# Delta on 32-partition blocks, three modulation rows at once, an earlier second-norm guess in a one-core Mamba and expert layer

## The reference, cut to what matters

```python
mod = (silu(c) @ wmod).reshape(4, 6, 1, -1)          # six rows of 512 per batch
sa, ca, ga, sb, cb, gb = (mod[:, i] for i in range(6))
h = layernorm(x) * (1 + ca) + sa
# the mixer
x_conv = causal_depthwise_conv(h, conv_w, conv_b)     # 4 taps
p = h @ Wxproj.T                                      # 2*128 + 1 columns
B, C = p[..., :128], p[..., 128:256]
delta = softplus(p[..., 256:])                        # one number per token
deltaA = exp(-exp(A_log) * delta)                     # 128 states
Bu = delta * B * (x_conv @ Winproj.T)
hs = scan(deltaA, Bu)                                 # hs[t] = deltaA[t]*hs[t-1] + Bu[t]
x = x + ga * ((C * hs) @ Woutproj.T + D * x_conv)     # ga clamped to |ga| >= 0.25
# the experts: each token goes to one of two
h = layernorm(x) * (1 + cb) + sb
x = x + gb * top_weight * expert[argmax](h)           # fc to 2048, leaky square, proj to 512
```

## Time and profile before

| | |
|---|---|
| time, median of 3 runs | 548.8 us (548.78 to 552.28) |
| the profiled execution | 548.64 us |
| its span, first to last instruction | 546.9 us |
| TensorE busy, share of the span | 508.2 us, 93% |
| VectorE busy | 351.1 us, 64% |
| ScalarE busy | 261.2 us, 48% |
| GpSimd busy | 159.4 us, 29% |
| mean granted TensorE clock | 0.974 |

### The profile page before, as it was taken

The page is one execution under the profiler, slowest core; times in us unless marked ns, Lnnn a source line. Parts: engine busy times, 40 slices in busy tenths (PEclk is TensorE's granted clock), DMA queues, the critical chain, the costliest instruction groups (busy, mean ns, idle before and its releaser), DMA issues.

```text
span 546.9 us, 7697 instructions
## 1 busy us (share of the span) xinstructions
PE 508.2 (93%) x2280; PEld 387.3 (71%) x2280; DVE 351.1 (64%) x734; ACT 261.2 (48%) x520; POOL 159.4 (29%) x204
## 2 busy tenths in 40 slices
PE   7899899999398999999999999999999999999990
PEld 1354355545276888898888888888888888988880
DVE  4688999898998675464445354545454544668781
ACT  2763387946786743443443344344346334433220
POOL 1100003030334520330150033034004304868583
PEclk9999999999778999999999999999999999999995
DMA  8930442220042004030022022002102300467692
GB/s 297 427 126 0 139 171 77 78 78 1 2 135 99 4 3 156 20 136 2 1 78 79 1 78 79 1 1 91 67 1 78 117 1 4 115 120 179 81 164 96
DMA packets 15729, 46.29 MB, mean 85 GB/s; under 512 B 5223, under 2 KB 5223, under 8 KB 12344
## 3 DMA queue, kind: packets, MB, share of 16 engines
q1 hardware_dynamic: 10600, 34.71, 17.8%
q0 software_dynamic: 5072, 10.79, 9.5%
HBM read 37.30 MB, written 8.71 MB: 84 GB/s over the span
## 4 chain that ended last, share of the span: by engine, by line
PE 71%; DVE 18%; issue 4%; ACT 3%; DMA 1%; DVEq 1%; POOL 1%; ACTq 0%; SPq 0%; POOLq 0%
PE bank L1200 34%; PE bank L1169 32%; DVE xc L1327 4%; DVE res L1365 2%; DVE st L1372 1%; PE bank L992 1%; DMA x_in<-x 1%; DVE st L1309 1%; ACT XSfull L769 1%; DVE eabs L1389 1%; DVE hs L1355 1%; PE bank L1006 1%; PE bank L1016 1%; DVE XSfull L1607 1%; PE bank L1033 1%
## 5 line engine op out<-in xcount | busy, mean ns | idle before, releaser
L565 POOL TENSOR_TENSOR Wlo<-raw,Whi (+1 forms) x60 | 76.3, 1301 | 227.7 <-ACT Whi L911 219.1
L1630 DVE TENSOR_TENSOR acc<-acc,bank 128x512 f32<-128x512 f32 x110 | 74.9, 687 | 57.2 <-PE bank L1200 57.2
L1614 DVE TENSOR_TENSOR twice_h<-twice_h,bank 128x512 f32<-128x512 f32 (+2 forms) x80 | 48.2, 606 | 95.5 <-ACT twice_h L882 95.5
L1169 PE MATMUL bank<-XShi,Wlo 128*128 x304 | 108.1, 355 | 0.0
L1169 PE MATMUL bank<-XSlo,Whi 128*128 x304 | 108.0, 355 | 0.0
L1169 PE MATMUL bank<-XShi,Whi 128*128 x304 | 108.0, 355 | 0.0
L1200 PE MATMUL bank<-Whi,ahi 128*128 128x512 f32 x268 | 105.2, 393 | 2.1 <-DVE alo L1620 2.1
L1200 PE MATMUL bank<-Wlo,ahi 128*128 128x512 f32 x268 | 105.2, 393 | 0.0
L1200 PE MATMUL bank<-Whi,alo 128*128 128x512 f32 x268 | 104.9, 392 | 0.0
L891 ACT ACTIVATE ahi<-twice_h 128x512 fp32r<-128x512 f32 (+2 forms) x78 | 44.6, 572 | 118.9 <-PE bank L1200 118.9
L882 ACT ACTIVATE twice_h<-bank 128x512 f32<-128x512 f32 (+2 forms) x78 | 41.4, 534 | 85.5 <-PE bank L1169 76.2
(11 more groups left out here) (197 smaller groups left out, 579.1 us busy)
## 6 DMA issues: line engine op xcount, KB each, us to landing
raw<-wffn SPq DMA_DIRECT2D x16, 1024.0 KB, 5.2
wm<-wmod SPq DMA_DIRECT2D x6, 1024.0 KB, 12.8
out<-res SPq DMA_DIRECT2D x4, 1024.0 KB, 4.5
x_in<-x SPq DMA_DIRECT2D x3, 1024.0 KB, 12.3
ga_bc<-ga_rows SPq DMA_DIRECT2D x4, 256.0 KB, 3.6
x<-x SPq DMA_DIRECT2D x1, 1024.0 KB, 5.3
bc<-router_rows_scaled SPq DMA_DIRECT2D x4, 256.0 KB, 3.6
wx_sb<-wx SPq DMA_DIRECT2D x1, 514.0 KB, 8.5
```

The source lines that it names most:

```text
L565: pool.tensor_tensor(Wlo[:, hb % 2, c, :], raw[:, c, :], Whi[:, hb % 2, c, :].bitcast(F32), ALU.subtract).then_inc(s_wlo, 1)
L1169: mm = pe.matmul(hP[(par + u) % 2][m][:, c0:c1], W[wp][:, par, 2 * e + k // 2, o:o + P], XS[xp][:, k, bass.ds(start_row[u] + c0, c1 - c0)] ...
L1614: dve.tensor_tensor(twice_h[:, m, 0:w], twice_h[:, m, 0:w], hP[(par + u) % 2][m][:, 0:w], ALU.add).then_inc(s_q2[m], 1)
L1630: dve.tensor_tensor(acc[:, n, :], acc[:, n, :], yP[s][:, :], ALU.add).then_inc(s_yu, 1)
```

## The change: what it does

1. `delta_product` puts the 512 tokens of a batch on four blocks of 32 partitions: 16 matmuls of 32x128, each at a column group of its own, into the first 128 columns of `pD`. Its weights are the column of `Wxproj` read with step 0, so `wdb` and the instructions that build it are gone.
2. Abs, Exp, `w1`, the residue, Ln and the two last steps work on 128x128 and end in `sp`.
3. A new `spread_delta` on TensorE: four matmuls of 128x128, with one column of the identity repeated as weights, take each block of `sp` back to all partitions in `pD`. ScalarE copies `pD` into `delta`, now a tile of its own, ahead of the exp in `decay`.
4. `last_mod_rows` makes rows 3, 4 and 5 together, in turns over `k`, at column groups 0, 32 and 64 of one bank. The single rows 3, 4 and 5 go. `turn(3)` moves behind `C_product(1)`; `mod_columns` for both move ahead of `softplus(1)` on VectorE.
5. On ScalarE `exp_minus_abs(1)` moves ahead of `guess1(2)`, `normalize1(2)` behind two of the row copies, and `guess2(1)` and `guess2(2)` between the last two blocks of `place`.
6. On TensorE `spread_delta(b + 1)` stands behind the state product of that batch, and the delta product of batch 3 moves from the end of batch 1's turn to between the second and third skip product of batch 2.

```diff
-        lw = take("lw", [P, L])
-        delta = lw
+        delta = take("delta", [P, L])
...
-        row_bank = (pO[0], pX, pO[0], pT[0], pT[1], pO[1])
-        col_bank = (pO[1], pO[1], pO[1], pT[0], pT[1])
+        row_bank = (pO[0], pX, pO[0], pT[0], pT[0], pT[0])
+        row_tile = (0, 0, 0, 0, 32, 64)
+        col_bank = (pO[1], pO[1], pO[1], pT[1], pT[1])
...
-                act.activation(eabs[:, :], pD[:, :], ACT.Abs).then_inc(s_ab, 1)
+                act.activation(eabs[:, 0:P], pD[:, 0:P], ACT.Abs).then_inc(s_ab, 1)
                 act.wait_ge(s_ab, b + 1)
-                act.activation(eabs[:, :], eabs[:, :], ACT.Exp, scale=-1.0).then_inc(s_u, 1)
+                act.activation(eabs[:, 0:P], eabs[:, 0:P], ACT.Exp, scale=-1.0).then_inc(s_u, 1)
 
             def log_part(b):
                 act.wait_ge(s_w1, 2 * b + 2)
-                act.activation(lw[:, :], w1[:, :], ACT.Ln).then_inc(s_lw, 1)
+                wait(act, s_sd, b)
+                act.activation(sp[:, :], w1[:, 0:P], ACT.Ln).then_inc(s_lw, 1)
 
             def decay(b):
+                act.wait_ge(s_sd, b + 1)
+                wait(act, s_bu, b)
+                act.activation(delta[:, :], pD[:, :], ACT.Copy).then_inc(s_dl, 1)
                 act.wait_ge(s_dl, b + 1)
                 act.activation(dA[:, :], delta[:, :], ACT.Exp, scale=Acol[:, 0:1]).then_inc(s_dA, 1)
...
+            exp_minus_abs(1)
             guess1(2)
-            exp_minus_abs(1)
             diagonals(1)
             log_part(1)
-            normalize1(2)
             mod_row_copy(3)
             mod_row_copy(4)
+            normalize1(2)
+            mod_row_copy(5)
             decay(1)
             guess2(0)
             modulate1(2, (0, 1))
...
-            place(0, (2, 3))
+            place(0, (2,))
+            guess2(1)
+            place(0, (3,))
             decay(2)
             modulate1(3, (2, 3))
-            guess2(1)
...
+            def last_mod_rows():
+                for r in (3, 4, 5):
+                    pe.wait_ge(s_wm[r], 16)
+
+                pe.wait_ge(s_hT, KT * 2)
+                for k in range(KT):
+                    for r in (3, 4, 5):
+                        mm = pe.matmul(row_bank[r][row_tile[r]:row_tile[r] + NB, :], sc[:, NB * k:NB * k + NB], wm[r][:, k, :],
+                                       start=(k == 0), stop=(k == KT - 1), tile_position=(0, row_tile[r]))
+                        if k == KT - 1:
+                            mm.then_inc(s_mm, 1)
...
                     pe.wait_ge(s_hT, KT * b + k + 1)
-                    mm = pe.matmul(pD[:, :], wdb[:, k, :], hT[b % 2][:, k, PAD:PAD + L], start=(k == 0), stop=(k == KT - 1))
+
+                    for j in range(TJ):
+                        o = QUARTER * j
+                        mm = pe.matmul(pD[o:o + QUARTER, 0:P], wx_sb[:, k, 2 * S:2 * S + 1].broadcast_to([P, QUARTER]), hT[b % 2][:, k, PAD + P * j:PAD + P * j + P],
+                                       start=(k == 0), stop=(k == KT - 1), tile_position=(0, o))
                 mm.then_inc(s_pd, 1)
+
+            def spread_delta(b):
+
+                pe.wait_ge(s_sp, b + 1)
+                for j in range(TJ):
+                    mm = pe.matmul(pD[:, P * j:P * j + P], ident[:, QUARTER * j:QUARTER * j + 1].broadcast_to([P, P]), sp[:, :], start=True, stop=True)
+                mm.then_inc(s_sd, 1)
...
+            spread_delta(0)
             state_product(0)
...
+                for n, j in enumerate(ORDER[:3]):
+                    if n == 2 and b == 2:
+                        delta_product(3)
                     skip_product(b, j)
...
                     delta_product(1)
-                    mod_rows(3)
-                    mod_rows(4)
-                    turn(3)
+                    last_mod_rows()
...
                     C_product(b + 1)
                 if b == 0:
+                    turn(3)
                     turn(4)
...
-                if b == 2:
-                    mod_rows(5)
                 if nxt:
                     state_product(b + 1)
+                    spread_delta(b + 1)
                 if b + 2 < NB:
                     transposes1(b + 2, (2, 3))
-                    delta_product(b + 2)
+                if b == 0:
+                    delta_product(2)
                 prefix(b)
...
                 dve.wait_ge(s_lw, b + 1)
-                own.link(dve.tensor_tensor(lw[:, :], lw[:, :], eabs[:, :], ALU.subtract))
-                dve.scalar_tensor_tensor(delta[:, :], pD[:, :], 0.0, lw[:, :], ALU.max, ALU.add).then_inc(s_dl, 1)
+                own.link(dve.tensor_tensor(sp[:, :], sp[:, :], eabs[:, 0:P], ALU.subtract))
+                dve.scalar_tensor_tensor(sp[:, :], pD[:, 0:P], 0.0, sp[:, :], ALU.max, ALU.add).then_inc(s_sp, 1)
```

More of the change, by code:

```diff
@@ L36 @@
 TJ = L // P
+QUARTER = P // TJ
 UNITS = (4, 4, 4, 3, 2)
@@ L213, in build @@
         gap = const("gap", [P, META])
-        wdb = const("wdb", [P, KT, P])
+        sp = const("sp", [P, P])
         c_sb = const("c_sb", [P, KT * NB])
@@ L337, in build @@
         s_mm = sem("mod_row_done")
-        s_wdb = sem("delta_weights_ready")
         s_Dga = sem("D_ga_ready")
@@ L369, in build @@
         s_lw = sem("log_ready")
+        s_sp = sem("softplus_ready")
+        s_sd = sem("delta_spread_done")
         s_dl = sem("delta_ready")
@@ L672, in mod_row_copy @@
                     act.wait_ge(s_wdr, 1)
-                act.activation(mod_row[r % 2][:, :], row_bank[r][0:NB, :], ACT.Identity,
+                act.activation(mod_row[r % 2][:, :], row_bank[r][row_tile[r]:row_tile[r] + NB, :], ACT.Identity,
                                bias=1.0 if r in (0, 3) else 0.0).then_inc(s_rw[r], 1)
@@ L842, in _ @@
             log_part(3)
-            place(1, (1, 2, 3))
+            place(1, (1, 2))
+            guess2(2)
+            place(1, (3,))
             decay(3)
-            mod_row_copy(5)
-            guess2(2)
             normalize2(2)
@@ L977, in transposes1 @@
                     wait(pe, s_e0, KT * (TJ * (b - 3) + k + 1))
-                    if b == 2 and k < 2:
-                        pe.wait_ge(s_cols, 3 + k)
+                    if b == 2 and k == 0:
+                        pe.wait_ge(s_rw[5], 1)
+                    if b == 2 and k == 1:
+                        pe.wait_ge(s_cols, 4)
                     wait(pe, s_hT, KT * b + k - 1)
@@ L1075, in _ @@
             transposes1(0, (2, 3))
-            pe.wait_ge(s_wdb, 1)
+            pe.wait_ge(s_wt, 48)
             delta_product(0)
@@ L1086, in _ @@
                 nxt = b + 1 < NB
-                for j in ORDER[:3]:
+                for n, j in enumerate(ORDER[:3]):
+                    if n == 2 and b == 2:
+                        delta_product(3)
                     skip_product(b, j)
@@ L1335, in softplus_residue @@
                 dve.wait_ge(s_u, b + 1)
-                dve.tensor_scalar(w1[:, :], eabs[:, :], 1.0, None, ALU.add).then_inc(s_w1, 1)
+                dve.tensor_scalar(w1[:, 0:P], eabs[:, 0:P], 1.0, None, ALU.add).then_inc(s_w1, 1)
                 dve.wait_ge(s_w1, 2 * b + 1)
-                own.link(dve.scalar_tensor_tensor(eabs[:, :], w1[:, :], -1.0, eabs[:, :], ALU.add, ALU.subtract))
+                own.link(dve.scalar_tensor_tensor(eabs[:, 0:P], w1[:, 0:P], -1.0, eabs[:, 0:P], ALU.add, ALU.subtract))
                 dve.sem_inc(s_w1, 1)
@@ L1432, in mod_columns @@
                 o = KT * NB * (r % 3)
-                dve.wait_ge(s_mc, r + 1)
+                dve.wait_ge(s_mc, r + 1 if r < 3 else 5)
                 dve.tensor_copy(cols[:, n, :, :].rearrange("p k b -> p (k b)"), col_bank[r][:, o:o + KT * NB]).then_inc(s_cols, 1)
@@ L1518, in _ @@
             dve.tensor_scalar(Acol[:, :], Acol[:, :], -1.0, None, ALU.mult).then_inc(s_An, 1)
-            dve.wait_ge(s_wt, 48)
-            for k in range(KT):
-                ins = dve.tensor_scalar(wdb[:, k, :], ones[:, :], wx_sb[:, k, 2 * S:2 * S + 1], None, ALU.mult)
-                if k < KT - 1:
-                    own.mark(ins)
-                else:
-                    ins.then_inc(s_wdb, 1)
             taps = {}
@@ L1577, in _ @@
                         router_row(True)
+                        mod_columns(3, 3)
+                        mod_columns(4, 4)
                     softplus(b + 1)
@@ L1582, in _ @@
                 if b == 0:
-                    mod_columns(3, 3)
-                    mod_columns(4, 4)
                     router_row(False)
```

6 lines of the change are left out of this document (removed).

## The result

The changed kernel takes 544.7 us (median of 12 runs, 542.9 to 547.7) where the kernel before took 548.9 in the same comparison: a ratio of 0.9916 with a 95% interval of 0.9891 to 0.9941, 4.3 us or 0.8% less. On another chip it was 544.8 against 549.0, 0.9929 (0.9898 to 0.9961). The forecast was 543.4.

What follows compares the result with a forecast made beforehand. VectorE was taken to set the time from 50 us to the mixer's end, TensorE a step behind; shifts of -3.0, -4.3 and finally -5.2 us over three turns gave 548.64 - 5.2 = 543.4, range 541.0 to 549.5.

Steps and rivals of the forecast that it cites:

- D + M: TensorE's delta product (D) plus three modulation rows (M): half overlap of column groups, 1.9 and 5.5 us, 7.4 together.
- rival (a): Column groups overlap fully, D = 1.0, M = 3.9; VectorE limits batch 0's turn; -6.3, 542.3 us; chance 0.22.
- (b): Column groups run one after another on TensorE, D = 3.74, M = 10.3; sum +0.5, 549.1 us; chance 0.10.
- (d): Column tiles cost more than they save, weight loads stand open, D = 6.4, M = 12.5; 556.7 us; chance 0.08.
- Softplus and the copies: Per batch: VectorE's four instructions 0.22 + 3 x 0.29 us, saving 1.4; ScalarE's delta copy 0.58; TensorE's spread 0.94.
- The first turn: Batch 0's turn: TensorE's path puts the mask at 73.8 us, -3.0, and binds, not VectorE's -3.6.
- Batch 2's turn: VectorE gains another -0.6 and -0.75 for -5.65; TensorE's path puts Bu(3) at 124.2 us; taken as -5.2.
- rival (c): ScalarE becomes the bound, decay waiting for the spread; three turns each lose 1 us, 546.4 us; chance 0.10.
- signs of being wrong: Column groups not overlapping, VectorE's Bu waiting for ScalarE's decay, or the transposes waiting for the mod row 5 copy.
- the term of -0.47: Batch 1's turn: the second norm's guess, now between two placed blocks on ScalarE, gives -0.47 us by batch 2's Bu.
- gets no case of its own: TensorE's clock: still busy 23 of about 25 us, so a fall in the mixer was given no separate case.
- a pure shift: After Bu(3) the stretch to 148 us and the expert stage keep their length and only start earlier.

Runs made afterwards that it cites:

- experiment 7: Changed kernel with the same matmuls reordered, each column group's matmuls all in a row before the next group's; one execution, 551.4 us.
- second profile: Profile of another execution of the changed kernel, unedited, from its repeat on another chip: 544.83 us, span 543.1; the repeat's median 544.8 us, ratio 0.9929.
- Experiment 4: Changed kernel with the exponential of batch 1's margin ahead of normalize2(1) on ScalarE: 542.1 us, ratio 0.9891 (0.987 to 0.9912).
- first profile: Profile of one execution of the changed kernel, among the longest of its 12 times: 547.68 us, span 545.9.
- experiment 9: Kernel before with only the second norm's guess of batches 1 and 2 moved ahead of the last placed block: 550.8 us, ratio 1.0023.
- experiment 5: Changed kernel with only guess2(1) and guess2(2) put back behind the placed blocks, decay and modulate: 550.0 us, ratio 0.9991.
- experiment 10: Kernel before with only the delta and softplus change, modulation rows one by one and guess in its old place: 555.6 us, ratio 1.011.
- experiment 3: Changed kernel with eight idle 128x512 matmuls filling TensorE's pauses: 543.1 us, ratio 0.9909 (0.9882 to 0.9936).

## Why the prediction came out as it did

**The time.** 543.4 was forecast, 544.7 measured; but the way there holds two errors that partly cancel (column groups priced too dear, about 1.1 us; a wait of 2.7 to 2.9 us not seen) and one term whose meaning was wrong. So part of the nearness is luck.

**Column groups: the term D + M was mis-sized.** I took the middle, 1.9 and 5.5 us, since the two records of one matmul share a group. Measured 1.08 and 3.61: full overlap, the size of rival (a), and rivals (b) and (d) fall with it. The next group's matmul doesn't wait for the second record of the one before it; with the alternation that the change writes the overlap is full, without it about half (experiment 7). The Trainium skill's measured speedup of 2.38 for three column tiles ("TensorE: Matmul & The Clock Gate", Part 3) would have made the rows an estimated 4.3 us (10.3 / 2.38); here three rows took 3.61 against 10.3 in single file, 2.9 times. The drain that the Trainium skill names at a change of tiling mode ("TensorEngine Tiling (Array Packing)", Key Properties) is about a tenth of a microsecond here, if it is there at all: batch 3's delta product, with skip products of the full array on both sides, takes its 1.08 us, and the eight skip records behind it 1.16 instead of 1.05 (rows below).

TensorE's timeline in the second profile:

```profile
99.01 2.08 PE L1063 MATMUL bank<-diag,xc 128*128 128x128 f32 x16
101.01 1.08 PE L1016 MATMUL bank<-hT,wx_sb 128*32 128x128 f32 x32
102.02 1.16 PE L1063 MATMUL bank<-diag,xc 128*128 128x128 f32 x8
```

**Softplus and the copies: right.** 0.22 and three of 0.28 to 0.29 were forecast and measured; the copy of delta 0.58 for 0.58, ScalarE's short ones 0.27 to 0.31 for 0.35, the spread 1.05 for 0.94.

**The first turn: right, for another reason.** Batch 0's mask came at 73.09 and 73.64; the forecast was 73.8 with TensorE's chain as the limit. With the shorter D and M, VectorE was the limit, as rival (a) had it (-3.6). The wait for batch 1's exponential went, and its residue began at 49.70 for 49.85. Batch 2's residue at 80.95 and 81.51 is 1.2 and 0.7 us ahead of the forecast, again rival (a)'s step.

**Batch 2's turn: the failed step.** I gave this turn another -1.35 for VectorE and took the smaller of its path and TensorE's. The second profile lost 2.8 us there: it enters 5.1 us early at Bu(2) and is 2.3 early at batch 3's residue. No step asked when ScalarE would deliver the exponential of batch 1's margin, because the earlier trace rows shows no wait for it. In the kernel before it ended at 107.52, 0.8 us ahead of its reader:

```profile
107.33 0.19 ACT L736 ACTIVATE eal<-al 128x4 f32<-128x4 f32 x1
```

```profile
108.35 0.16 DVE L1426 TENSOR_SCALAR den<-eal 128x4 f32<-128x4 f32 x1
```

A VectorE 4 us earlier runs into it. This is rival (c)'s mechanism, ScalarE as the bound, at one place for 2.7 to 2.9 us instead of three places of 1 us. What I held against it, 4.4 us of air in ScalarE's stretch, was beside the point: ScalarE has air, but its order ties a 0.2 us instruction to placed blocks that come at TensorE's pace. Experiment 4 takes this wait away and lands at 542.1, where rival (a) stood at 542.3. One of my own signs of being wrong came in part: in the first profile Bu(2) waited 1.4 us for ScalarE's copy of delta, in the second it did not. And TensorE's chain was priced too long here, by more than the product: C began at 109.2 and 108.2 us for 110.6, and Bu(3) of experiment 4 at 122.73, where I had 124.2 for TensorE's path.

**The guess: the term of -0.47 was a misreading.** I priced the move by the wait that it ends in the kernel before. Alone it gains nothing (experiment 9); in the changed kernel its absence costs the whole gain (experiment 5: 4.8 and 2.3 us of waiting). The walk had the guess already in its new place for batches 1 and 2, ahead of decay, and so the total holds it rightly. The same walk with the guess left behind decay would have shown the dependence: I had written that decay now waits for the spread and that guess2 queues behind it, and had put that in the sum for batch 0's turn only. In batch 2's turn of experiment 10 that queue kept VectorE waiting for 7.9 us.

**The clock: "gets no case of its own" was wrong.** The argument was TensorE's mean busy share, 23 of about 25 us. The faster TensorE pauses more: 2.44 us at 68 and 1.9 to 2.2 at 73, where its longest pauses in this stretch had been 1.59 (at 67.50) and 0.67 (at 77.01); the clock over 65 to 80 us was 0.67 and 0.89. The stretch's mean hid the pause. In the first profile this cost 1.4 us at Bu(2), and the two profiles' lengths differ by 1.0 us at Bu(3), in part through it. How much of the median it takes stays open: experiment 3 removes the fall and gains at most 1.6 us, inside the intervals.

**After Bu(3), a pure shift: right in the second profile.** 39.15 us to the projection there, 39.17 before; 40.23 in the first, with the subtractions that collided, and 0.8 us more behind the projection. The joint wait for the three wmod loads cost nothing, as forecast: no idle time stands before the rows.

## What to carry to other kernels

That the profile before shows no wait doesn't mean that there is room: before an engine is made some microseconds faster, read for each of its inputs how long before the reader the writer is done, because the smallest of these margins is the next limit (here 0.8 us of margin turned into 2.9 of waiting). The parts of such a change can't be priced by the waits that each ends, or tried one by one and dropped: the same 0.4 us of ScalarE work, moved, was worth nothing alone and some 4 us in company. When an engine gets less work, look at its longest pause and not at its busy share.

## What the runs showed of the hardware

Matmuls in different column groups overlap completely when neighbours in the queue alternate between groups: three float32 products of 512 columns in 3.61 us, as long as one; four groups of 128 columns in 1.08 instead of 3.74. Going from the full array to groups and back cost 0.1 us at most in the one place read (1.16 for 1.05 us). With all matmuls of a group in a row they still overlap by about half (7.04 and 2.46 us, one execution): the next group's first record starts with the fifth of the eight before it, ahead of records that stand earlier in the queue. TensorE's granted clock fell to the lower level (1.2 GHz) behind a pause of 2.44 us in one execution, and only behind the next pause, of 2.15 us, in another execution of the same kernel (a skip product of 5.47 and of 4.55 us, 2.97 at the full clock); with both pauses filled it stayed at 1.00. VectorE's four subtractions of 128x512 took 3.60 us when GpSimd's started 1.5 to 1.8 us behind their start (five profiles), and 2.50 when it started later (nine).
